# A gated graph network on 64 batches: rows of the first group in two transfers, and a reordered last frame

## What is computed

```python
for _ in range(3):
    a  = adj @ h                                  # per batch, used twice: av = [a, a]
    z  = sigmoid(lin(av, w3) + lin(h, u3))
    r  = sigmoid(lin(av, w4) + lin(h, u3))
    hv = tanh(lin(av, w5) + lin(r * h, u5))
    h  = (1 - z) * h + z * hv
out = layernorm(x + h)
```

## Time and profile before

| | |
|---|---|
| Median of 3 runs | 761.15 us (760.79 to 761.39) |
| The profiled execution's own time | 761.69 us |
| Its span, first to last instruction | 758.8 us |
| Mean granted TensorE clock | 0.995 |
| Busy: PE, DVE, ACT, POOL | 746.4, 544.5, 388.7, 72.8 us |
| Transfers to landing: group rows 512 KB, y 512 KB, y 256 KB | 4.9, 2.7, 2.0 us (medians) |

### The profile page before, as it was taken

How to read it: one execution, slowest core, us unless ns; L and a number is a source line. 1 busy time by engine, 2 the same in 40 slices (tenths; PEclk the granted TensorE clock), 3 DMA queues, 4 the chain that set the end, 5 groups by cost and what they waited for, 6 DMA issues and landing times.

```text
span 758.8 us, 10474 instructions
## 1 busy us (share of the span) xinstructions
PE 746.4 (98%) x3681; PEld 632.4 (83%) x3681; DVE 544.5 (72%) x858; ACT 388.7 (51%) x647; POOL 72.8 (10%) x91
## 2 busy tenths in 40 slices
PE   9999999999999999999999999999999999999994
PEld 7888888888888888888888888888888888888883
DVE  6657787777767776887677667887677756887675
ACT  5545454455556444545566544545466645444454
POOL 0000111100100011110100001120000000211003
PEclk9999999999999999999999999999999999999998
DMA  8122312233453322223355242222335432111222
GB/s 309 33 38 37 90 28 34 39 44 80 117 123 67 103 39 38 39 37 58 63 121 134 67 92 32 38 33 35 64 63 130 125 66 38 30 31 31 43 45 103
DMA packets 208425, 51.82 MB, mean 68 GB/s; under 512 B 201232, under 2 KB 201360, under 8 KB 208400
## 3 DMA queue, kind: packets, MB, share of 16 engines
q1 hardware_dynamic: 208256, 51.24, 31.3%
q10 hardware_dynamic: 144, 0.26, 0.1%
HBM read 18.95 MB, written 8.39 MB: 36 GB/s over the span
## 4 chain that ended last, share of the span: by engine, by line
PE 98%; DVE 1%; DMA 1%; POOL 0%; issue 0%; ACT 0%; ACTq 0%; SPq 0%; POOLq 0%
PE ps_g L327 17%; PE ps_g L326 17%; PE ps_g L328 17%; PE ps_a L351 11%; PE ps_v L326 11%; PE ps_v L327 11%; PE ps_v L328 11%; PE ps_g L408 1%; DMA x_in<-in_x_rows 1%; PE ps_v L408 0%; DVE dz L648 0%; DVE hT L658 0%; DVE dz L643 0%; PE ps_a L482 0%; DVE stats L756 0%
## 5 line engine op out<-in xcount | busy, mean ns | idle before, releaser
L523 ACT ACTIVATE ps_v<-ps_v,bias 128x512 f32<-128x512 f32 x96 | 63.6, 662 | 199.9 <-PE ps_v L328 199.9
L328 PE MATMUL ps_g<-aT_hi,wt_hi 128*128 128x512 f32 x376 | 146.3, 389 | 0.0
L326 PE MATMUL ps_g<-aT_hi,wt_lo 128*128 128x512 f32 x376 | 146.3, 389 | 0.0
L327 PE MATMUL ps_g<-aT_lo,wt_hi 128*128 128x512 f32 x376 | 146.3, 389 | 0.0
L643 DVE TENSOR_TENSOR dz<-ps_v,hT 128x512 f32<-128x512 f32 x64 | 44.3, 692 | 103.6 <-ACT ps_v L523 103.6
L553 ACT CAST rh_hi<-rh 128x512 fp32r<-128x512 f32 x96 | 59.6, 621 | 78.1 <-DVE rh L663 78.1
L561 ACT ACTIVATE z<-ps_g,bias 128x512 f32<-128x512 f32 x96 | 64.2, 687 | 47.5 <-PE ps_g L328 46.4
L638 DVE TENSOR_TENSOR aT_lo<-ps_a,aT_hi 128x512 fp32r<-128x512 f32 x96 | 62.4, 673 | 28.9 <-ACT aT_hi L508 28.8
L328 PEld LDWEIGHTS ps_g<-aT_hi,wt_hi 128*128 128x128 f32 x376 | 70.6, 188 | 14.6
L326 PEld LDWEIGHTS ps_g<-aT_hi,wt_lo 128*128 128x128 f32 x376 | 70.6, 188 | 14.6
L327 PEld LDWEIGHTS ps_g<-aT_lo,wt_hi 128*128 128x128 f32 x376 | 70.6, 188 | 14.6
(11 more groups left out here) (78 smaller groups left out, 1185.2 us busy)
## 6 DMA issues: line engine op xcount, KB each, us to landing
hn<-hb SPq DMA_DIRECT2D x736, 32.0 KB, 2.0
x_in<-in_x_rows SPq DMA_DIRECT2D x16, 512.0 KB, 4.9
xT<-in_x_cols SPq DMA_DIRECT2D x15, 512.0 KB, 4.4
out<-y SPq DMA_DIRECT2D x15, 512.0 KB, 2.7
wide<-in_w_t SPq DMA_DIRECT2D x3, 512.0 KB, 6.0
xT<-in_x_cols SPq DMA_DIRECT2D x2, 256.0 KB, 4.7
out<-y SPq DMA_DIRECT2D x2, 256.0 KB, 2.0
square<-in_u_t ACTq DMA_DIRECT2D x1, 256.0 KB, 2.8
```

The source lines that it names most:

```text
L326: nc.tensor.matmul(dst, lhs_lo, rhs_hi, start=first, stop=False, skip_group_check=True)
L327: nc.tensor.matmul(dst, lhs_hi, rhs_lo, start=False, stop=False, skip_group_check=True)
L328: return nc.tensor.matmul(dst, lhs_hi, rhs_hi, start=False, stop=last, skip_group_check=True)
L523: nc.scalar.activation(ps_v[:, oc, :], ps_v[:, oc, :], ACT.Tanh, bias=bias[:, BV, oc:oc + 1]).then_inc(v_ready, 1)
```

## The change

At the start, the rows of group 0 come as two transfers of 256 KB with a semaphore each (`rows_first`), the first aggregation waits for each half where it needs it, and `keep_warm` issues 20 transposes in place of 17.

In the loop, the z products of a round's last frame stand at the head of the next pass and no longer at the end of the pass. In the last frame:

- TensorE: transposes of group 14, candidate of group 15, then its z products, then its transposes, by chunk and half. Batches 0 and 1 of group 15 go to a bank of `ps_g[0]`, batches 2 and 3 to the two banks of `ps_v` (`y_bank`).
- ScalarE: tanh comes before z; z of chunk 1 is evaluated in two pieces of 256 columns; then y of group 14, y of group 13, and three of the four batches of group 15 into a buffer of its own (`y_tail`).
- VectorE: statistics of group 14, then of group 13, both subtractions, then multiplication and addition for chunk 0 and for the two halves of chunk 1; statistics and the addition of epsilon by halves; the fourth batch of group 15 is normalised here.
- GpSimd: groups in the order 12, 14, 13; for group 15 only `neg_mean`, `rstd` and `shift`.
- SyncE: stores in the order 12, 14, 13, 15.

```diff
@@ sync
-            load_rows(0, 0)
+            for hf in range(2):
+                part = slice(hf * HB, (hf + 1) * HB)
+                sp.dma_start(x_in[0][:, part, :], x_rows[:, part, :]).then_inc(rows_first[hf], DMA)
...
-            for q in range(SLOTS - 1):
+            for q in (0, 2, 1):
                 store(last, q)
             for hf in range(2):
                 part = slice(hf * HB, (hf + 1) * HB)
-                sp.wait_ge(normed[SLOTS - 1], GB * last + HB * (hf + 1))
+                sp.wait_ge(tail_normed[hf], HB)
                 sp.dma_start(out_rows[:, B - GB + hf * HB:B - GB + (hf + 1) * HB, :],
-                             y[1][:, part, :]).then_inc(stored[1], DMA)
+                             y_tail[:, part, :]).then_inc(tail_stored, DMA)
@@ tensor
                 for hf in range(2):
+                    if first:
+                        pe.wait_ge(rows_first[hf], DMA)
...
                 value(i, j, carry)
-                gate_z(i, j)
+                if j < FR - 1:
+                    gate_z(i, j)
...
-                keep_warm(17)
+                keep_warm(20)
...
             with nc.Fori(1, ROUNDS, engines=(pe.engine,), hint_back_edge=True) as i:
+                gate_z(i - 1, FR - 1)
                 first_half(i, 0, True)
...
+            def last_output(c, hf):
+                for b in range(hf * HB, (hf + 1) * HB):
+                    done = nc.tensor.transpose(y_bank(SLOTS - 1, b)[:, c * P:(c + 1) * P],
+                                               hT[SLOTS - 1][:, c, b * N:(b + 1) * N], ident[:, :])
+                if c == C - 1:
+                    done.then_inc(y_transposed, 1)
...
             candidate(last, FR - 1)
+            gate_z(last, FR - 1)
             pe.wait_ge(z_ready, C * frames(last, FR - 2))
-            for c in range(C):
-                pe.wait_ge(h_ready, C * frames(last, FR - 1) - 1 + c)
-                output(SLOTS - 1, c, ps_g[0])
+            pe.wait_ge(d_ready, C * frames(last, FR - 1))
+            pe.wait_ge(tail_h, 1)
+            for hf in range(2):
+                last_output(0, hf)
+            for hf in range(2):
+                pe.wait_ge(tail_h, hf + 2)
+                last_output(1, hf)
@@ scalar
+            tanh_v(last, j)
+            def last_z(oc, rows):
+                act.wait_ge(zpre_ready, C * frames(last, j) - 1 + oc)
+                nc.scalar.activation(z[1][:, oc, rows], ps_g[1][:, oc, rows], ACT.Sigmoid,
+                                     bias=bias[:, BZ, oc:oc + 1]).then_inc(tail_z, 1)
+            last_z(0, slice(0, ROWS))
+            for hf in range(2):
+                last_z(1, slice(hf * HALF, (hf + 1) * HALF))
...
+            normalise(last, 1)
             q = SLOTS - 1
+            for hf, batches in enumerate(((0, 1), (2,))):
                 act.wait_ge(shift_ready[q], last + 1 + hf)
+                for b in batches:
+                    nc.scalar.activation(y_tail[:, b, :], y_bank(q, b), ACT.Identity,
+                                         bias=shift[q][:, b:b + 1], scale=rstd[q][:, b:b + 1])\
+                      .then_inc(tail_normed[hf], 1)
@@ vector
+            for hf in range(2):
+                last_statistics(SLOTS - 2, hf)
+            statistics(last, 1)
             for c in range(C):
+                v_minus_h(last, j, c)
+            def last_h(c, rows, nth):
+                dve.wait_ge(d_ready, C * frames(last, j) - 1 + c)
+                dve.wait_ge(tail_z, nth)
+                nc.vector.tensor_tensor(dz[:, c, rows], dz[:, c, rows], z[1][:, c, rows], ALU.mult).then_inc(tail_zd, 1)
...
+            last_h(0, slice(0, ROWS), 1)
+            for hf in range(2):
+                last_h(1, slice(hf * HALF, (hf + 1) * HALF), hf + 2)
+            q = SLOTS - 1
+            for hf in range(2):
+                last_statistics(q, hf)
+                last_var_eps(q, hf)
+            b = GB - 1
+            dve.wait_ge(rstd_ready[q], last + 2)
+            nc.vector.tensor_scalar(y_tail[:, b, :], y_bank(q, b),
+                                    meanvar[q][:, b, 0:1], rstd[q][:, b:b + 1],
+                                    ALU.subtract, ALU.mult).then_inc(tail_normed[1], 1)
```

More of the change, by code:

```diff
@@ L116, in build @@
         y = [sb(f"y{k}", [P, GB, D]) for k in range(2)]
+        y_tail = sb("y_tail", [P, GB, D])
         hT_hi = sb("hT_hi", [P, C, ROWS], F32R)
@@ L155, in build @@
         x_loaded = [sem(f"x_loaded{k}") for k in range(2)]
+        rows_first = [sem(f"rows_first{hf}") for hf in range(2)]
         stored = [sem(f"stored{k}") for k in range(2)]
@@ L192, in build @@
         h_ready = sem("h_ready")
+        tail_zpre, tail_z, tail_zd, tail_h = sem("tail_zpre"), sem("tail_z"), sem("tail_zd"), sem("tail_h")
+        tail_normed = [sem(f"tail_normed{hf}") for hf in range(2)]
+        tail_stored = sem("tail_stored")
         pool_passed, dve_passed = sem("pool_passed"), sem("dve_passed")
@@ L208, in turn, with rows_loads @@
             return SLOTS // 2 * i + (q // 2 + 1)
+        def rows_loads(i, q):
+            return DMA * (turn(i, q) - (1 if q % 2 == 0 else 0))
         def xT_loads(i, q):
@@ L336, in dense, with aggregate @@
                 return done
-            def aggregate(i, j):
+            def aggregate(i, j, first=False):
                 q = j % SLOTS
-                if j < SLOTS:
-                    pe.wait_ge(x_loaded[q % 2], DMA * turn(i, q))
+                if first:
+                    pass
+                elif j < SLOTS:
+                    pe.wait_ge(x_loaded[q % 2], rows_loads(i, q))
                 else:
@@ L451, in first_round @@
                 pe.wait_ge(ident_ready, 1)
-                keep_warm(17)
+                keep_warm(20)
                 pe.wait_ge(adjT_loaded, DMA)
-                aggregate(0, 0)
+                aggregate(0, 0, first=True)
                 first_u()
@@ L595, in _ @@
             last = ROUNDS - 1
-            frame(last, FR - 1, False, None)
-            tanh_v(last, FR - 1)
-            normalise(last, 1)
+            j = FR - 1
+            tanh_v(last, j - 1)
+            normalise(last, 0)
+            for oc in range(C):
+                act.wait_ge(rpre_ready, C * frames(last, j) - 1 + oc)
+                nc.scalar.activation(r_sb[:, oc, :], ps_g[1][:, oc, :], ACT.Sigmoid,
+                                     bias=bias[:, BR, oc:oc + 1]).then_inc(r_ready, 1)
+            for oc in range(C):
+                act.wait_ge(rh_ready, C * frames(last, j) - 1 + oc)
+                nc.scalar.copy(rh_hi[:, oc, :], rh[:, oc, :]).then_inc(rh_hi_ready, 1)
+            tanh_v(last, j)
[6 more added lines that the diff above has]
+                last_z(1, slice(hf * HALF, (hf + 1) * HALF))
             q = SLOTS - 2
@@ L749, in _, with last_statistics @@
             last = ROUNDS - 1
-            frame(last, FR - 1, True, None)
-            def last_statistics(q, src, hf):
+            j = FR - 1
+            v_minus_h(last, j - 1, 0)
+            times_z(last, j - 1, 0)
+            v_minus_h(last, j - 1, 1)
+            new_h(last, j - 1, 0)
+            times_z(last, j - 1, 1)
+            new_h(last, j - 1, 1)
+            for c in range(C):
+                times_r(last, j, c)
+            rh_low(last, j, 0)
+            rh_low(last, j, 1)
+            def last_statistics(q, hf):
                 dve.wait_ge(y_transposed, 2 * (q - (SLOTS - 2)) + hf + 1)
                 for b in range(hf * HB, (hf + 1) * HB):
-                    nc.vector.bn_stats(stats[q][:, b, :],
-                                       by_batch(src[:, hf, :])[:, b % HB, :]).then_inc(stats_ready[q], 1)
+                    nc.vector.bn_stats(stats[q][:, b, :], y_bank(q, b)).then_inc(stats_ready[q], 1)
                 dve.wait_ge(stats_ready[q], GB * last + HB * (hf + 1))
@@ L811, in _ @@
             last = ROUNDS - 1
-            for q in range(SLOTS - 1):
+            for q in (0, 2, 1):
                 scale_and_shift(last, q, in_loop=False)
+            q = SLOTS - 1
             for hf in range(2):
-                scale_and_shift(last, SLOTS - 1, slice(hf * HB, (hf + 1) * HB), hf + 1, in_loop=False)
+                part = slice(hf * HB, (hf + 1) * HB)
+                pool.wait_ge(meanvar_ready[q], GB * last + HB * (hf + 1))
+                nc.gpsimd.tensor_scalar(neg_mean[q][:, part], meanvar[q][:, part, 0], -1.0, None,
+                                        ALU.mult).then_inc(neg_mean_ready[q], 1)
+                pool.wait_ge(var_eps_ready[q], last + hf + 1)
+                nc.gpsimd.tensor_tensor(rstd[q][:, part], var_eps[q][:, part], neg_half[:, part],
+                                        ALU.pow).then_inc(rstd_ready[q], 1)
+                pool.wait_ge(rstd_ready[q], last + hf + 1)
+                pool.wait_ge(neg_mean_ready[q], last + hf + 1)
+                nc.gpsimd.tensor_tensor(shift[q][:, part], neg_mean[q][:, part], rstd[q][:, part],
+                                        ALU.mult).then_inc(shift_ready[q], 1)
```

34 lines of the change are left out of this document (19 added, 15 removed).

## The result

| | before | changed |
|---|---|---|
| time, median (range, executions) | 761.0 us (760.1 to 762.37, 8) | 758.43 us (757.88 to 758.89, 8) |
| ratio, with its 95% interval | | 0.9965 [0.9955, 0.9976] |
| profiled execution: own time / span | 761.69 / 758.8 us | 758.45 / 755.8 us |

What follows compares the result with a forecast made beforehand. TensorE holds 98% of the chain of waits, so only what precedes its first useful matmul or follows its last can gain. Start 0, loop 0 and end -2.5 us gave a median of 758.6 us, range 757.2 to 759.8.

Steps and rivals of the forecast that it cites:

- The start, 0: Start: halved rows and three more fillers put the first aggregation at 5.86 us, for 0 gain, bounds -0.1 and +0.1.
- The states' high part: cover of over 1 us: Start: casts at 6.38 and 7.0, wanted after 8 us; without that cover the first gate waits some 0.4 us.
- Rival (a): Start: closing the 0.36 us gap makes TensorE's clock rise earlier, 0.85 us less or more, time 757.7; chance 0.22.
- Steps 1 and 2: Last frame: transposes at G, tanh 2.44 after the first, candidate at G + 0.88, then z; z pieces 0.51 us each.
- G: Last frame's reference time: start of TensorE's last z products before (740.48), first transpose of group 14 in the changed kernel.
- Step 3: Last frame: VectorE's statistics and two subtractions end at 746.63, after z of chunk 0, so VectorE sets the pace.
- Step 4: Last frame: VectorE's four 256-element operations on chunk 1 take 0.42 us each, ending at 749.7; two whole ones, 749.42.
- Steps 5 and 6: Tail: split hides transposes, statistics start at 749.7; epsilon on VectorE 0.2, root to y 1.09, last piece ends 753.85.
- Steps 7 and 8: Tail: ScalarE's queue clears 0.1 us in time, last y piece 2.5 us earlier, last store keeps its 2.46.
- The sum: Whole kernel: start 0, loop 0, end -2.5; 759.2 us for the profiled execution, 758.6 for the median.
- rival (b): Tail: thin covers, queued stores and dearer half pieces cost about 1.1 us, some 0.9 at the end: 759.5; chance 0.15.
- Rival (d): Loop's head: instructions fetched late after the branch idle TensorE at three crossings, 1.5 us each giving 763.1; chance 0.03.

Runs made afterwards that it cites:

- e2: Changed kernel with the start of before (rows of group 0 in one transfer, 17 fillers), so the end's edits without the start's: 758.02 us, ratio to before 0.9956.
- e1: Kernel before with only the start's edits (rows of group 0 in two halves, 20 fillers): 761.1 us, ratio to before 0.9998.
- e3: Changed kernel with 17 fillers again, rows still in halves: 758.25 us, ratio to before 0.9959.
- e4: Changed kernel with the rows of group 0 in one transfer again, 20 fillers kept: 758.81 us, ratio to before 0.9963.
- e9: Kernel before with only the z products of a round's last frame moved to the loop's head: 760.1 us, ratio to before 0.9991.
- e10: Changed kernel run again, unedited, in a later set: 758.63 us, ratio to before 0.998.
- e5: Changed kernel with chunk 1 of group 15 whole again, not split in two: 758.76 us, ratio to before 0.9972.
- e6: Changed kernel with z ahead of group 14's transposes and the candidate on TensorE, and ahead of tanh on ScalarE, again: 760.16 us, ratio to before 0.9986.
- e7: Changed kernel with the epsilon addition back on GpSimd and the fourth y piece back on ScalarE: 759.44 us, ratio to before 0.9987.
- e8: Changed kernel with group 13's store in two halves and group 15's last half stored in two quarters: 758.14 us, ratio to before 0.9966.
- e11: Same program as e4 run again (changed kernel, rows in one transfer, 20 fillers): 758.53 us, ratio to before 0.9984.

## Why the prediction was right, point by point

- **What bounds it.** Right: in the middle nothing moved (19.41 to 19.07 and 188.81 to 188.47 are the same shift), and the gain is the end's (e2).
- **The start, 0.** Right for the median (e1 0.9998; e2, e3, e4 within a few tenths of the changed kernel). In the profile it was -0.34, outside the step's bounds of 0.1, by chance as far as e9 shows. The reasons were thinner than the text says. "The states' high part: cover of over 1 us" was wrong: the columns behind the halved rows came later, and the casts ran at 7.18 and 8.06 instead of 6.38 and 7.0 (with halved rows the first cast began at 6.82 to 7.44 in seven profiles of eight and at 6.07 in e3, with whole rows at 6.38 to 6.95). The cover was 0.16 us in the changed kernel's profile (cast ends 7.80, product 7.96) and below nothing in e1 and e10 (0.23 and 0.26 us of idle time). The step named a price of some 0.4 if it was gone; these two are what came.
- **Rival (a).** It fell as a cause. The spacing halves early or late with the gap and without it: with a gap at 7.5 us (before), between 5.4 and 5.9 (e9), and only behind the aggregation (e2); without one at 6.7 us (changed), 6.1 (e10), 5.6 (e1) and ahead of 4.96 (e3). The same program twice gave 6.7 and 6.1. So the prediction read from one execution a moment that moves by more than 2 us from one to the next.
- **Steps 1 and 2 (TensorE's order, tanh, z).** Right: tanh 2.50 behind the first transpose (2.44), no stall of the candidate, z at G + 5.23 (5.17). The candidate began at G + 0.83; for the 0.88 of the prediction no row stands (in the trace of before it was 0.79), and the low part was done 0.14 ahead of it. The half pieces of z took 0.42, under the lower bound of 0.51 that a piece of y gave.
- **Step 3, "VectorE sets the pace, not ScalarE".** Wrong: the subtractions ended at G + 5.82 instead of G + 6.15 (0.20 of it in the statistics ahead, 0.13 in the two subtractions, 1.25 us and not 1.38), and the multiplication waited 0.20 for ScalarE's z. So it is the chain of TensorE's z products and ScalarE's z that sets this moment; on the sum the error is 0.13, since the multiplication began at G + 6.02.
- **Step 4, 0.42 for 256 elements.** Right: 0.42 in all four. So the formula of the Trainium skill ("VectorE: DVE Perf Modes", the section on the TRN2 errata) agrees with the trace, 0.424 against 0.42; its advice to keep tiles at 512 elements or more did not decide here, since the split hides another engine's step (e5). The four halves ended 0.25 later than two whole ones do in e5, by the formula it would be 0.31.
- **Steps 5 and 6.** Statistics at G + 8.95 (9.22), the second ones 1.15 after the first (1.24), epsilon 0.17 (0.2), root to y 1.03 (1.09), one piece 0.56 (0.51). All small and mostly in one direction: end at G + 13.01 instead of G + 13.37.
- **Steps 7 and 8, the covers.** ScalarE's queue was clear at 751.34, the first tail piece started at 751.45: the cover of 0.1 held. VectorE's own piece took 0.54 and hid. The store's distance grew from 2.46 to 2.64, inside the 0 to 0.3 and not the 0 that was taken. Of rival (b) that is all that came (its 1.1 is the sum of four terms, not of three).
- **The sum.** -2.5 forecast; the median span fell by 2.3 to 2.9, by which of the sets one takes, the time by 2.3 (e10) and 2.6. That 758.43 lies within 0.2 of 758.6 is in part luck. For the profiled execution the forecast was 759.2 and it took 758.45: the end gave 2.85 and not 2.5, the start's chance 0.34, the stores took 0.18, and the time outside the span was 2.65 instead of 2.9. The mechanism was right; the number was closer than its terms.
- **Rival (d).** Fell at the loop's head (e9). But TensorE without cause to wait was seen at the loop's exit, in e1 and e4, which the prediction had not looked at.

## What to carry to other kernels

In a serial tail, put the product with the longest chain behind it first, and give each step to the engine that is idle there: the order on TensorE was worth about 1.8 us here (an estimate from e6), moving two small operations off the last engines about 1 (e7), the split 0.4 or less (e5). These are the prices of taking one part back from the changed kernel; they sum to more than the 2.85 of the whole, so each depends on the others. The new order of the stores and of y had no run of its own. Split an operation only where its first half lets another engine begin, and count what the queue puts behind a split transfer. Judge a start by many executions: the same start gave 18.54, 19.41 and 20.96 in three profiles.

## What the runs showed of the hardware that had not been expected

- **TensorE idle behind the loop's exit, now and then.** 2.57 us with nothing released in e4's profile, 0.29 in e1's. Many of the long executions stand near two steps, spans some 2.3 to 2.6 us over the others (e4: 757.9 to 758.2; e8: 758.2) and some 4.6 to 5 over (e11: 759.8 to 760.4; e10: 760.6), which would fit one or two such stalls; others lie between or beyond (e5 759.1, e7 759.5 and 761.1, three of before 760.0, 760.6 and 760.8), and only e4's is seen in a trace. That instructions arrive late there was only argued; no run tested it, and whether some programs have it more often, and why, stays open.
- **Time outside the span depends on the program.** 1.73 to 1.81 us in all 11 executions of e6 and 1.75 to 1.84 in those of e9, a median near 2.6 for most others, and 2.0 to 2.1 or 2.9 to 3.3 by turns in e2, e3, e4 and e11. It can hide or feign 0.8 us. Its cause is open; comparing spans leaves it out.
- **TensorE's level at the start.** The granted clock reads 1.00 in every stretch of the first 12 us of the kernel before (the earlier trace rows is one of them), while the spacing of 0.22 us, twice the 0.11 that follows, shows the 1.2 GHz level until 5 to 10 us in these profiles. Two executions of the same program changed to the short spacing at 6.7 and 6.1 us. At the start the spacing tells, the column doesn't.
- **TensorE's level at the end.** The level falls again in the tail, and there the column shows it. In the kernel before it fell behind the last transposes (granted clock 1.00 up to 751.5, then 0.50), in e1, e9 and e6 ahead of them. Where it fell first, the statistics came 0.19 to 0.24 us later. TensorE had stood idle 1.66 and 1.33 us ahead of the two groups of transposes in before and in e1 alike, so these idle times alone do not decide it.
